# A second edge stage on one Trainium2 core: the order of a group's matrix products on TensorE, and squares in two parts

## The chip, the core and the metric

The kernel runs on one core of one Trainium2 chip. Its time is the device time of one execution in microseconds (us), here the median of three runs. A core has TensorE (PE: matrix products, and PEld: its weight loads), VectorE (DVE), ScalarE (ACT), GpSimd (POOL), SyncE (SP) and DMA engines. Each engine works through its own list of instructions, and the lists meet in semaphores.

## What is computed

The reference is a graph network of two layers over 6250 nodes and 106250 edges. The change lies in the second layer's edge stage alone. Its part of the reference, cut to what matters:

```python
h = silu(edge_scalars @ fc_w1 * (1 / sqrt(8))) * SILU_NORM       # first layer of the edge weights
w = h @ fc_w2 * (1 / sqrt(64))                                   # second layer: 256 weights an edge
w_a, w_b, w_c, w_d = w[:, :64], w[:, 64:128], w[:, 128:192], w[:, 192:]
xg0, xg1 = y0[edge_src], y1[edge_src]                            # gathered rows
mid0 = w_a * xg0 * ea0
mid1 = w_b * einsum('euc,ec->eu', xg1, ea1) * INV_SQRT3
mid2 = (w_c * xg0)[:, :, None] * ea1[:, None, :]
mid3 = (w_d * ea0)[:, :, None] * xg1
agg = segment_sum(concatenate([mid0, mid1, mid2, mid3]), edge_dst)
```

Beside it, in the same stage, run the keys and values of the layer's linear attention: `k, v` of 512 columns each are projected, normalised by their squares' sums, and `dots = k^T v` is summed over all nodes.

## The kernel before

`edges1` runs this stage. 106250 edges are taken in 139 **groups** of 768 edges (six tiles of 128, that is three pairs). The function `turns` writes the first ten groups out, then a loop whose iteration holds ten groups (11 iterations, groups 10 to 119), then the last 19 groups. `q` is a group's place in a turn of five. Groups 0 to 124 also carry a chunk of 250 nodes in five groups: the key and value products (`products`) stand in `q` = 0 to 3, `gram` of the chunk before in `q` = 0 and 2, and none of it in `q` = 4. Groups from 125 on carry no chunk.

In the step of group g each engine does this, in this order:

- **POOL** gathers six tiles of rows three groups ahead, when ACT has copied their indices (`stage`).
- **ACT**: `stage(g+3)`; `attributes(g+1)` (L2084) copies the turned edge scalars out of PSUM; `squares` (L2105, L2109) copies a key or value product out and squares it by head, eight activations each with a read of its accumulator; `copied(g-1)` (L2098) copies the sums of group g-1 to `us`; `silu(g+1)` (L2090); where it is due, `root` (L2114) and `scaled` (L2120). Sqrt and Silu lie in different tables, so that a load of a table stands before the silu that follows a root.
- **DVE**: `eq` (L2192) and `oh` (L2200), the one-hot matrix of the destinations times the attributes; the messages of pair 0, 1 and 2 (L2213 and twice L2215); the three additions of group g-2's step (`add(g-1)`, L2172), after PE's `flip`; the small operations of the normalisation (L2176, L2178, L2183).
- **PE**: `second(g,0)` (L2269, the weight product of pair 0, on 64 rows of the array), `front(g+1)` (L2249, turns the scalars), the first half of `sums(g-1)` (L2283, 24 products of 32 columns), `second(g,1)`, the second half of `sums(g-1)`, `first(g+1)` (L2255), `second(g,2)`, `flip(g-1)` (L2293, which waits for ACT's `us`), then `products` (L2306) and `gram` (L2313).

The weights of pairs 0 and 2 lie in PSUM banks 0 and 1 of `pW`, those of pair 1 in banks 2 and 3, beside `iota` and `eq`. So `second(g,0)` waits until all messages of g-1 are made and until `silu(g)`; `second(g,1)` until `oh(g)` has read `eq`; `second(g,2)` until message 0 of g has read bank 0 and 1. `sums(g-1)` wait for the messages of g-1 and for the additions of g-2.

Of the kernel before, what the change touches and what calls it, by code (L numbers as in the profile page):

```python
# [46 lines left out]
SUB, W1, ST = 3, 32, 2  # L47
# [1913 lines left out]
def edges1(env, z):  # L1961
# [5 lines left out]
    PAIRS = T1 // 2  # L1967
    QW = SUB * W1
    HID = 512
    with ExitStack() as ctx:  # L1970
# [45 lines left out]
        def in_chunks(hi):  # L2016
            return hi < LAST
# [4 lines left out]
        def one_pass():  # L2022
            with nc.Block() as block:
# [49 lines left out]
                @block.scalar  # L2073
                def _(act):
                    def stage(g, s, lo):
                        if lo >= PER:
                            hold(act, s_msg, PAIRS * (g - PER + 1))
                            nc.scalar.copy(ix[:, s, :], srcI[:, bass.ds(g * T1, T1)]).then_inc(s_ix, 1)

                    def attributes(g, s, lo):  # L2080
                        if lo >= 2:
                            hold(act, s_F, g - 1)
                        hold(act, s_T, g + 1)
                        nc.scalar.copy(esT[:, s % 2, :], pT).then_inc(s_esT, 1)  # L2084

                    def silu(g, s, lo):
                        if lo >= 2:
                            hold(act, s_W, PAIRS * (g - 1))
                        hold(act, s_F, g + 1)
                        nc.scalar.activation(hT[:, s % 2, :, :],  # L2090
                                             pH[:, 0:128 * PAIRS].rearrange("p (i e) -> p i e", e=128)[:, :, 0:P],
                                             ACT.Silu, scale=8.0 ** -0.5).then_inc(s_h, 1)

                    def copied(g, lo):
                        if lo >= 1:
                            hold(act, s_flip, g)
                        hold(act, s_acc, g + 1)
                        nc.scalar.copy(us[:, :], pU[0:QW, :]).then_inc(s_us, 1)  # L2098

                    def squares(c, n, lo):  # L2100
                        t, b = n // 2, n % 2
                        if lo >= PER:
                            hold(act, s_gram, 2 * c - 1 + t)
                        hold(act, s_kv, 4 * c + n + 1)
                        nc.scalar.copy((kc, vc)[b][0:R, t, :], pKV[0:R, :]).then_inc(s_cp, 1)  # L2105
                        act.wait_ge(s_cp, 4 * c + n + 1)
                        for h in range(8):
                            head = pKV[0:R, 64 * h:64 * h + 64]
                            last = nc.scalar.activation(head, head, ACT.Square, accum_out=(ssk, ssv)[b][:, t, h:h + 1])  # L2109
                        last.then_inc(s_read, 1)  # L2110

                    def root(c, t):
                        hold(act, s_ab, 2 * c + t + 1)
                        nc.scalar.activation(sd[:, t, :], ab[:, t, :], ACT.Sqrt).then_inc(s_sd, 1)  # L2114

                    def scaled(c, t):
                        hold(act, s_ri, 2 * c + t + 1)
                        hold(act, s_read, 4 * c + 2 * t + 2)
                        for h in range(8):
                            last = nc.scalar.activation(vc[0:R, t, 64 * h:64 * h + 64], vc[0:R, t, 64 * h:64 * h + 64],  # L2120
                                                        ACT.Copy, scale=ri[:, t, h:h + 1])
                        last.then_inc(s_vs, 1)

                    def step(g, r, lo, hi, c):
                        q = r % PER
                        if lo == 0:
                            nc.scalar.activation(ta[0:1, 0:1], env["ones"][0:1, 0:1], ACT.Silu)
                            attributes(0, 0, 0)
                            silu(0, 0, 0)
                        if hi <= GROUPS1 - 4:  # L2130
                            stage(g + 3, (q + 3) % PER, lo + 3)
                        if hi <= GROUPS1 - 2:
                            attributes(g + 1, r + 1, lo + 1)
                        if in_chunks(hi) and q >= 1:
                            squares(c, q - 1, lo)
                        if lo >= 1:
                            copied(g - 1, lo - 1)
                        if hi <= GROUPS1 - 2:
                            silu(g + 1, r + 1, lo + 1)
                        if behind_chunk(lo) and q == 0:  # L2140
                            root(c - 1, 1)
                        if behind_chunk(lo) and q == 1:
                            scaled(c - 1, 1)
                        if in_chunks(hi) and q == 3:
                            root(c, 0)
                        if in_chunks(hi) and q == 4:
                            scaled(c, 0)
                        for n in range(2):
                            if lo == LAST + 7 + 2 * n:
                                act.wait_ge(s_M, n + 1)  # L2150
                                nc.scalar.copy(kc[:, n, :], pKV[:, :]).then_inc(s_m1, 1)
                        if lo == LAST + 11:
                            act.wait_ge(s_G, 1)
                            nc.scalar.copy(env["g0"][:, :, :], pKV[:, :].rearrange("p (k c) -> p k c", k=2))
                        if lo == GROUPS1 - 1:
                            copied(g, lo)
                            act.drain()
                    turns(act, step)

                @block.vector  # L2160
                def _(v):
# [23 lines left out]
                    def step(g, r, lo, hi, c):  # L2185
                        q, s = r % PER, r % 2
# [15 lines left out]
                            in1=ea[:, q, :, :].unsqueeze(3).broadcast_to([P, T1, 4, W1]), op=ALU.mult).then_inc(s_oh, 1)  # L2202
                        bases = []
                        v.wait_ge(s_gat[q], (c + 1) * 16 * T1)
                        for i in range(PAIRS):
                            if lo >= 1:
                                bases.append(base_of(g - 1, i))
                            js = slice(2 * i, 2 * i + 2)
                            v.wait_ge(s_W, g * PAIRS + i + 1)
                            wa = region(i).rearrange("p j (b q c) -> p j b q c", b=2, q=2)  # L2210
                            m = msg[:, s, js, :, :]
                            x0 = rows[:, q, js, 0:64].unsqueeze(2).broadcast_to([P, 2, 2, 64])
                            nc.vector.tensor_tensor(out=m[:, :, 0:8:7, :], in0=wa[:, :, :, 0, :], in1=x0, op=ALU.mult)  # L2213
                            for j in range(2):
                                last = nc.vector.tensor_tensor(  # L2215
                                    out=m[:, j, 1:7, :].rearrange("p (b q) c -> p b q c", b=2), in0=wa[:, j, :, 1:2, :].broadcast_to([P, 2, 3, 64]),
                                    in1=rows[:, q, 2 * i + j, 64:256].rearrange("p (q c) -> p q c", q=3).unsqueeze(1)
                                    .broadcast_to([P, 2, 3, 64]), op=ALU.mult)
                            last.then_inc(s_msg, 1)
# [24 lines left out]
                def _(pe):  # L2244
# [14 lines left out]
                    def second(g, r, lo, i):  # L2259
                        if i == 0:  # L2260
                            pe.wait_ge(s_h, g + 1)
                            if lo >= 1:
                                pe.wait_ge(s_msg, g * PAIRS)
                        elif i == 1:
                            pe.wait_ge(s_oh, g + 1)
                        else:
                            pe.wait_ge(s_msg, g * PAIRS + 1)
                        for n in range(2):
                            last = nc.tensor.matmul(region(i)[:, n, :], hT[64 * n:64 * n + 64, r % 2, i, :],  # L2269
                                                    w2[64 * n:64 * n + 64, :], start=True, stop=True)  # L2270
                        last.then_inc(s_W, 1)
# [67 lines left out]
                    def step(g, r, lo, hi, c):  # L2339
                        q = r % PER  # L2340
                        if lo == 0:
# [2 lines left out]
                                             skip_group_check=True)  # L2344
                            front(0, 0, 0, 0)
                            first(0, 0)
                        second(g, r, lo, 0)
                        if hi <= GROUPS1 - 2:
                            front(g + 1, (q + 1) % PER, lo + 1, c + (1 if q == PER - 1 else 0))
                        if lo >= 1:  # L2350
                            sums(g - 1, r + 1, lo - 1, 0)
                        second(g, r, lo, 1)
                        if lo >= 1:
                            sums(g - 1, r + 1, lo - 1, 1)
                        if hi <= GROUPS1 - 2:
                            first(g + 1, r + 1)
                        second(g, r, lo, 2)
                        if lo >= 1:
                            flip(g - 1)
                        if in_chunks(hi) and q < 4:  # L2360
# [722 lines left out]
```

## Time and profile before

| what | value |
|---|---|
| time, median of 3 runs | 4415.78 us (4412.92 to 4420.58) |
| profiled execution, span from first to last instruction | 3329.5 us |
| median less span | 1086.3 us |
| second edge stage (windows view, from the first `oh` to the last addition) | 1171.54 us |
| busy in the span: PE, PEld, DVE, ACT, POOL | 2844.0, 2195.3, 2255.2, 1469.1, 1823.7 us |
| mean granted clock of PE | 0.935 |

The profile gives no time of its own for the profiled execution besides its span. What lies around the span is taken as 1086.3 us, the median less the span; the change doesn't touch it. In a row of a timeline the first number is the start, the second the duration, both in us, and what stands in brackets is the idle time of the engine before it and what ended it.

### The profile page before, as it was taken

To read this page: it belongs to the slowest core of one execution; us is meant where nothing else is said; L and a number is where in the kernel's file an instruction comes from. 1 tells how busy PE (TensorE), PEld (TensorE's weight loads), DVE (VectorE), ACT (ScalarE), POOL (GpSimd) and SP (SyncE) were. 2 spreads that over 40 slices of the span, in tenths; PEclk is the share of its full clock that TensorE was granted. 3 is DMA by queue.
4 is the path that set the end of the run, shared out by engine and by line. 5 is a ranking of instruction groups with operands and counts; after the bars stand their busy time and mean duration, and the time that the engine had idled before them with its cause. 6 is when DMAs were issued, how large, how long until landed. Compare 5 with 4: busy or idle time off the path is not lost. (4 is left out here: it accounts for less than half of the span.)

```text
span 3329.5 us, 78240 instructions
## 1 busy us (share of the span) xinstructions
PE 2844.0 (85%) x22774; PEld 2195.3 (66%) x22774; DVE 2255.2 (68%) x6176; ACT 1469.1 (44%) x4662; POOL 1823.7 (55%) x1961
## 2 busy tenths in 40 slices
PE   6787878788888788699996999999999999888399
PEld 4576667677777766588884555555555555578387
DVE  5577777777777777576665777777777777768522
ACT  5333333333333157333333665565555556348122
POOL 3577777777777601011115776666666667712254
PEclk9799999999999999899997999999999999999699
DMA  6544444444444557332224444344434444436221
GB/s 183 164 114 112 116 113 113 113 112 117 113 113 118 129 162 198 106 90 83 86 77 113 117 111 104 103 104 103 103 101 103 104 104 110 125 110 200 58 52 47
DMA packets 329958, 375.06 MB, mean 113 GB/s; under 512 B 179225, under 2 KB 236666, under 8 KB 329616
## 3 DMA queue, kind: packets, MB, share of 16 engines
q0 software_dynamic: 89712, 230.26, 25.3%
q1 hardware_dynamic: 238335, 139.99, 16.1%
q10 hardware_dynamic: 1696, 2.62, 0.2%
q14 instruction: 162, 1.32, 0.1%
q8 instruction: 53, 0.87, 0.1%
HBM read 309.90 MB, written 62.84 MB: 112 GB/s over the span
## 5 line engine op out<-in xcount | busy, mean ns | idle before, releaser
L2033 POOL DMA_INDIRECT e_rows<-tab,e_ix x804 | 759.9, 945 | 346.5 <-issue 218.1
L607 POOL DMA_INDIRECT e_rows<-tab,e_ix x805 | 761.3, 946 | 247.5 <-issue 217.2
L1008 PE MATMUL e_pU<-e_ohp,e_rows 128*128 128x128 f32 x3340 | 440.2, 292 | 3.1 <-DVE e_ohp L859 3.1
L1008 PEld LDWEIGHTS e_pU<-e_ohp,e_rows 128*128 128x128 f32 x3340 | 428.5, 209 | 4.8 <-DVE e_ohp L859 3.6
L2215 DVE TENSOR_TENSOR e_msg<-e_pW,e_rows 128x384 f32<-128x384 f32 x834 | 421.5, 547 | 0.0
L2269 PE MATMUL e_pW<-e_w,e_hT 64*128 64x256 f32 x1668 | 324.2, 438 | 76.3 <-DVE e_oh L2200 36.1
L2283 PE MATMUL e_pU<-e_msg,e_oh 128*32 128x128 f32 (+1 forms) x6672 | 374.8, 312 | 8.6 <-DVE sum L2172 7.5
L721 ACT CAST e_ohT<-e_pT 64x640 bf16<-64x640 f32 x167 | 114.4, 685 | 552.1 <-PE e_pT L989 551.8
L2213 DVE TENSOR_TENSOR e_msg<-e_pW,e_rows 128x256 f32<-128x256 f32 x417 | 175.4, 421 | 231.3 <-PE e_pW L2269 222.9
L2283 PEld LDWEIGHTS e_pU<-e_msg,e_oh 128*32 128x32 f32 x6672 | 243.4, 113 | 132.5 <-issue 72.4
L989 PE MATMUL e_pT<-ident,e_oh 128*64 128x128 f32 x835 | 135.5, 299 | 212.0 <-DVE e_oh L514 190.7
L989 PEld LDWEIGHTS e_pT<-ident,e_oh 128*64 128x64 f32 x835 | 89.9, 120 | 252.5 <-issue 248.8
L2269 PEld LDWEIGHTS e_pW<-e_w,e_hT 64*128 64x128 f32 x1668 | 148.3, 193 | 160.4 <-DVE e_msg L2215 64.7
L859 DVE TENSOR_TENSOR e_ohp<-window,e_p 128x1280 f32<-128x1280 f32 x167 | 245.8, 1472 | 0.1
L1699 POOL TENSOR_TENSOR m_rn<-m_ve,m_mhalf 125x2 f32<-125x2 f32 x50 | 45.6, 912 | 336.2 <-DVE m_ve L148 336.2
L2306 PE MATMUL e_pKV<-e_wkv,ffn_norm 128*125 128x512 f32 x400 | 206.2, 641 | 0.0
L1899 PE MATMUL m_pH<-m_xnT,m_w 128*128 128x250 f32 x800 | 175.4, 377 | 6.6 <-DMA m_w<-in_L_ffn_W 6.6
L1912 PE MATMUL m_pO<-m_w,m_hT 128*125 128x256 f32 x800 | 176.7, 379 | 0.0
L828 DVE TENSOR_TENSOR sum<-sum,e_pU 64x128 f32 x334 | 95.6, 286 | 119.4 <-issue 113.5
L2098 ACT COPY e_us<-e_pU 96x512 f32<-96x512 f32 x139 | 80.8, 581 | 213.6 <-PE e_pU L2283 210.3
L1899 PEld LDWEIGHTS m_pH<-m_xnT,m_w 128*128 128x128 f32 x800 | 151.1, 191 | 23.7 <-issue 6.7
L2109 ACT ACTIVATE e_pKV<-e_pKV 125x64 f32<-125x64 f32 x800 | 165.0, 237 | 3.2
(465 smaller groups left out, 5563.9 us busy)
## 6 DMA issues: line engine op xcount, KB each, us to landing
e_rows<-tab,e_ix POOLq DMA_INDIRECT x1609
xnT<-f_xnT SPq DMA_DIRECT2D x25, 250.0 KB, 2.9
e_xk<-xnT SPq DMA_DIRECT2D x25, 250.0 KB
xnT<-b_xT SPq DMA_DIRECT2D x25, 250.0 KB, 2.9
m_xnT<-xnT SPq DMA_DIRECT2D x25, 250.0 KB
xnT<-m_xT SPq DMA_DIRECT2D x25, 250.0 KB, 2.7
ffn_norm<-xnT SPq DMA_DIRECT2D x25, 250.0 KB
tab<-f_hrow SPq DMA_DIRECT2D x25, 227.5 KB
```

The lines of the kernel that those rows point to most:

```text
L607: nc.gpsimd.indirect_dma_start(out=rows[:, s, j, :], out_offset=None, in_=env["tab0"], in_offset=bass.IndirectOffsetOnAxis(ap=at[:, j:j + ...
L859: nc.vector.tensor_tensor(out=ohp[:, s % 3, :, :, :], in0=eq.unsqueeze(2).broadcast_to([P, GT, H0, W]), in1=p[:, s % 3, :, 0:H0].unsqueeze ...
L989: last = nc.tensor.transpose(pT[0:W, P * j:P * (j + 1)], oh[:, s, j, :], ident[:, :])
L1008: nc.tensor.matmul(pU[:, s % 2, 2 * W * k:2 * W * (k + 1)], rows[:, s, j, 128 * k:128 * k + 128], ohp[:, s % 3, j, 2 * k:2 * k + 2, :], st ...
L1899: last = nc.tensor.matmul(pH[:, f // 2, (f % 2) * CH:(f % 2 + 1) * CH], w1[:, j, k, 128 * c:128 * c + 128], xnT[:, s, k, :], start=k == 0, ...
L1912: last = nc.tensor.matmul(pO[:, t * C:(t + 1) * C], hT[:, s % 2, f, t * R:t * R + R], w2[:, f, :], start=f == 0, stop=f == NF - 1)
L2033: nc.gpsimd.indirect_dma_start(out=rows[:, r % PER, j, :], out_offset=None, in_=env["tab1"], in_offset=bass.IndirectOffsetOnAxis(ap=at[:, ...
L2213: nc.vector.tensor_tensor(out=m[:, :, 0:8:7, :], in0=wa[:, :, :, 0, :], in1=x0, op=ALU.mult)
L2215: last = nc.vector.tensor_tensor(out=m[:, j, 1:7, :].rearrange("p (b q) c -> p b q c", b=2), in0=wa[:, j, :, 1:2, :].broadcast_to([P, 2, 3 ...
L2269: last = nc.tensor.matmul(region(i)[:, n, :], hT[64 * n:64 * n + 64, r % 2, i, :], w2[64 * n:64 * n + 64, :], start=True, stop=True)
L2283: last = nc.tensor.matmul(u8[:, 0:8:2, :] if c == 0 else u8[:, 1:2 + 2 * c:2 * c, :], oh[:, r % 2, ST * i + j, c, :], m[:, 0:4, :] if c == ...
L2306: last = nc.tensor.matmul(pKV[0:R, :], xk[:, k, t * R:t * R + R], wkv[:, k, HID * b:HID * b + HID], start=k == 0, stop=k == 1)
```

## The change

On PE the three `second` of a group stand together at its start, in the order of pairs 0, 2, 1, then `front(g+1)`, both halves of `sums(g-1)`, `first(g+1)`, `flip(g-1)`, `products`, `gram`. The waits go with them: pairs 0 and 2 need messages 0 and 2 of g-1, pair 1 needs `oh(g)` and all messages of g-1. DVE makes the messages in the order 0, 2, 1, and waits for the second of PE's signals before the first two. On ACT `squares` is cut into `kept` (the copy) and `squares`; the copy and four heads come before `attributes(g+1)`, the other four after it. No operation is added or removed.

```diff
-                        if hi <= GROUPS1 - 2:
-                            attributes(g + 1, r + 1, lo + 1)
-                        if in_chunks(hi) and q >= 1:
-                            squares(c, q - 1, lo)
+                        chunk = in_chunks(hi) and q >= 1
+                        if chunk:
+                            kept(c, q - 1, lo)
+                            squares(q - 1, range(0, 4))
+                        if hi <= GROUPS1 - 2:
+                            attributes(g + 1, r + 1, lo + 1)
+                        if chunk:
+                            squares(q - 1, range(4, 8)).then_inc(s_read, 1)
...
-                        for i in range(PAIRS):
+                        for done, i in ((2, 0), (2, 2), (3, 1)):
                             if lo >= 1:
-                                bases.append(base_of(g - 1, i))
+                                bases.append(base_of(g - 1, len(bases)))
                             js = slice(2 * i, 2 * i + 2)
-                            v.wait_ge(s_W, g * PAIRS + i + 1)
+                            v.wait_ge(s_W, g * PAIRS + done)
...
                         if i == 0:
                             pe.wait_ge(s_h, g + 1)
                             if lo >= 1:
-                                pe.wait_ge(s_msg, g * PAIRS)
+                                pe.wait_ge(s_msg, g * PAIRS - 1)
                         elif i == 1:
                             pe.wait_ge(s_oh, g + 1)
-                        else:
-                            pe.wait_ge(s_msg, g * PAIRS + 1)
+                            if lo >= 1:
+                                pe.wait_ge(s_msg, g * PAIRS)
...
-                        second(g, r, lo, 0)
+                        for i in (0, 2, 1):
+                            second(g, r, lo, i)
                         if hi <= GROUPS1 - 2:
                             front(g + 1, (q + 1) % PER, lo + 1, c + (1 if q == PER - 1 else 0))
                         if lo >= 1:
-                            sums(g - 1, r + 1, lo - 1, 0)
-                        second(g, r, lo, 1)
-                        if lo >= 1:
-                            sums(g - 1, r + 1, lo - 1, 1)
+                            for j in range(ST):
+                                sums(g - 1, r + 1, lo - 1, j)
                         if hi <= GROUPS1 - 2:
                             first(g + 1, r + 1)
-                        second(g, r, lo, 2)
                         if lo >= 1:
                             flip(g - 1)
```

## Rows read from the trace of the kernel before

**Rows 1.** The page: the span, then two of the costliest groups of instructions.
```profile
span 3329.5 us, 78240 instructions
...
L2269 PE MATMUL e_pW<-e_w,e_hT 64*128 64x256 f32 x1668 | 324.2, 438 | 76.3 <-DVE e_oh L2200 36.1
...
L2109 ACT ACTIVATE e_pKV<-e_pKV 125x64 f32<-125x64 f32 x800 | 165.0, 237 | 3.2
```

**Rows 2.** Windows: stretch, its us, busy time (instructions), PEclk, DMA share, GB/s.
```profile
1779.86:2951.40 1171.54, 1083.55 (x10709) 668.16 (x10709) 853.88 (x2099) 655.64 (x2804) 786.62 (x833) 0.94 0.41 107
2043.53:2118.62 75.09, 70.00 (x730) 43.17 (x728) 55.23 (x138) 48.24 (x215) 51.43 (x55) 1.00 0.42 107
2118.62:2128.86 10.24, 9.44 (x46) 5.60 (x47) 6.57 (x16) 2.65 (x5) 5.37 (x7) 0.50 0.31 79
...
2203.95:2214.19 10.24, 9.44 (x46) 5.59 (x47) 6.57 (x16) 2.65 (x5) 5.56 (x7) 0.50 0.32 81
...
1825.07:1828.48 3.41, 3.29 (x28) 2.02 (x28) 2.66 (x6) 0.90 (x5) 2.50 (x3) 0.50 0.42 103
```

**Rows 3.** Waits of PE in ten iterations (1948 to 2801): in total, times, longest.
```profile
PE e_pW L2269 <- DVE e_oh L2200: 34.8, 20, 3.4
```

**Rows 4.** Timeline of PE: groups 38 and 39, and the start of iteration 40.
```profile
2104.78 0.55 PE L2293 MATMUL e_pU<-ident,e_us 96*128 96x96 f32 x4
2105.16 1.91 PE L2306 MATMUL e_pKV<-e_wkv,ffn_norm 128*125 128x512 f32 x4
...
2107.00 0.70 PE L2269 MATMUL e_pW<-e_w,e_hT 64*128 64x256 f32 x4
...
2107.86 1.29 PE L2283 MATMUL e_pU<-e_msg,e_oh 128*32 128x256 f32 x24
2109.07 0.70 PE L2269 MATMUL e_pW<-e_w,e_hT 64*128 64x256 f32 x4
...
2110.92 0.82 PE L2255 MATMUL e_pH<-e_esT,e_w 48*128 48x128 f32 x5
...
2112.22 0.55 PE L2293 MATMUL e_pU<-ident,e_us 96*128 96x96 f32 x4
2113.85 0.70 PE L2269 MATMUL e_pW<-e_w,e_hT 64*128 64x256 f32 x4 [1.08 <-ACT e_hT L2090]
...
2119.42 1.23 PE L2269 MATMUL e_pW<-e_w,e_hT 64*128 64x256 f32 x4 [3.26 <-DVE e_oh L2200]
```

**Rows 5.** Timeline of ACT and DVE in the same stretch.
```profile
2106.17 1.11 DVE L2172 TENSOR_TENSOR sum<-sum,e_pU 128x128 f32 x3
...
2107.69 0.96 DVE L2200 TENSOR_TENSOR e_oh<-e_pW,e_ea 128x768 f32<-128x768 f32 x1
...
2111.11 0.58 ACT L2098 COPY e_us<-e_pU 96x512 f32<-96x512 f32 x1 [0.53 <-PE e_pU L2283]
2111.94 1.28 ACT L2090 ACT_TABLE_LOAD   x1 [0.25 <-PE e_pH L2255]
...
2113.61 1.11 DVE L2172 TENSOR_TENSOR sum<-sum,e_pU 128x128 f32 x3
...
2118.01 0.36 DVE L2192 TENSOR_TENSOR e_pW<-e_pW,dst_rel 128x192 f32<-128x192 f32 x1 [2.96 <-issue]
2118.41 0.96 DVE L2200 TENSOR_TENSOR e_oh<-e_pW,e_ea 128x768 f32<-128x768 f32 x1
```

**Rows 6.** Timeline of PE and DVE in the middle of an iteration, groups 44 and 45.
```profile
2157.28 0.82 PE L2255 MATMUL e_pH<-e_esT,e_w 48*128 48x128 f32 x5
...
2159.97 1.12 DVE L2172 TENSOR_TENSOR sum<-sum,e_pU 128x128 f32 x3
...
2162.81 0.70 PE L2269 MATMUL e_pW<-e_w,e_hT 64*128 64x256 f32 x4 [0.18 <-DVE e_oh L2200]
```

**Rows 7.** Timeline at the stage's end: both halves of the last sums together, copy, flip.
```profile
2946.11 2.37 PE L2283 MATMUL e_pU<-e_msg,e_oh 128*32 128x256 f32 x48 [2.04 <-DVE sum L2172]
2949.22 0.55 PE L2293 MATMUL e_pU<-ident,e_us 96*128 96x96 f32 x4 [0.74 <-ACT e_us L2098]
...
2948.58 0.58 ACT L2098 COPY e_us<-e_pU 96x512 f32<-96x512 f32 x1 [5.11 <-PE e_pU L2283]
```

More of the change, by code:

```diff
@@ L2098, in copied, with kept @@
                         nc.scalar.copy(us[:, :], pU[0:QW, :]).then_inc(s_us, 1)
-                    def squares(c, n, lo):
+                    def kept(c, n, lo):
                         t, b = n // 2, n % 2
@@ L2106, in squares @@
                         act.wait_ge(s_cp, 4 * c + n + 1)
-                        for h in range(8):
+                    def squares(n, heads):
+                        t, b = n // 2, n % 2
+                        for h in heads:
                             head = pKV[0:R, 64 * h:64 * h + 64]
                             last = nc.scalar.activation(head, head, ACT.Square, accum_out=(ssk, ssv)[b][:, t, h:h + 1])
-                        last.then_inc(s_read, 1)
+                        return last
                     def root(c, t):
```

## The prediction

> **What bounds the kernel now.** I read the page first: the span, and the groups of L2269 and L2109, which the change moves [rows 1]. Then the windows view, to see the stage by itself: 1171.54 us, PE busy in 1083.55 of them, 92%, DVE in 73%; one iteration of the loop is 75.09 us at the full granted clock and 10.24 us at 0.50, 85.33 in all, and the next slow stretch starts 85.33 us after the last (2118.62, 2203.95) [rows 2]. So PE bounds most groups, and what it does not do itself must be sought in its waits. There the longest is for `oh`, 34.8 us in ten iterations [rows 3]. Then the timelines, to see where an iteration loses time.
>
> A group with `products` has no wait on PE. From one start to the next it takes 0.86 (pair 0 and front: 2107.00 to 2107.86), 1.21 (half the sums, to 2109.07), 1.85 (pair 1 and the other half, to 2110.92), 1.30 (first and pair 2, to 2112.22), and, from the group before, 0.38 (flip, 2104.78 to 2105.16) and 1.84 (products, to 2107.00): 7.44 us [rows 4]. A `gram` adds about 0.9 us, which the change leaves alone.
>
> A group with `q` = 4 has no products to cover anything. In group 39, the last of an iteration, PE waits 1.08 us for the silu, which had to load its table (1.28 us), then, past the loop's branch, 3.26 us for the next `oh` [rows 4, 5]. The reason for the second is DVE: it starts its additions at 2113.61, and its list stands still for 2.96 us, waiting for nothing that the profile shows, before 2118.01, the first instruction after the loop's branch [rows 5]. Inside those 3.26 us the granted clock falls to 0.50, for 10.24 us [rows 2].
>
> **The change part by part.** I count from F, the start of `first` in a group, on PE.
>
> Pairs 0, 2, 1 together: a pair takes 0.64, pair 1 and half the sums' 1.85 less the sums' 1.21 [rows 4]. Its own matmuls follow each other as they will in the new order, so three make 1.92, as now. No gain; what a switch between kinds of products could give beyond this is a rival below.
>
> Both halves of the sums together: the last sums of the stage already stand so, 48 products in 2.37 us [rows 7]. Apart a half is 1.21 to the next start and 1.29 to its own end (the row at 2107.86) [rows 4], so both make 2.50. Gain 0.13 a group.
>
> Flip behind first: at present pair 2 stands between them and flip starts at F + 1.30, when ACT's copy of the sums (2111.11 to 2111.69, F + 0.77) has long ended [rows 4, 5]. Now only first, 1.30 - 0.64 = 0.66, stands between. The row at the stage's end gives the wait that is then bare: 0.74 from the sums' end to flip, copy included [rows 7]. The sums end 0.07 after F (1.29 against 1.21), so flip starts at F + 0.81: a new wait of 0.15 on PE, behind which products, gram and the next group are queued. Its bounds are 0 (the switch from first to flip may take that long anyhow) and 0.25.
>
> Sum of a group with products: flip 0.81, products 0.38 + 1.84, pairs 0 and 2 1.28, pair 1 0.64, front 0.22 (0.86 - 0.64), sums 1.21 + 1.21 - 0.13: 7.46 against 7.44, **+0.02 us**. `oh` is not late here: additions to the end of `oh` take 2.48 (2106.17 to 2108.65) [rows 5]. They can start at flip's end plus what lies between in the rows, about 0.14, so at F + 1.50, and end at F + 3.98, while pair 1's turn comes at 0.81 + 0.38 + 1.84 + 1.28 = F + 4.31. The margin is 0.33.
>
> The loop's end: today DVE's additions start at F + 2.69 (2113.61 - 2110.92), because message 2 waits for pair 2. Afterwards they start at F + 1.50, 1.19 earlier, and from them to PE's start behind `oh` it is 5.81 (2113.61 to 2119.42) [rows 4, 5]. So PE resumes at F + 7.31 instead of F + 8.50. But then it has pair 1, front and both halves before the next F, 3.15, where it had 1.85. Together 10.46 against 10.35: **+0.11 us**. What the shorter wait gives, the work no longer done inside it takes back.
>
> The middle of an iteration (`q` = 4 without branch): from the additions to pair 1 it is 2.84 (2159.97 to 2162.81), so pair 1 starts at F + 4.34 and F' = F + 7.49; today it is 5.53 + 1.85 = 7.38 [rows 6]. **+0.11 us**.
>
> ACT: the same operations, four squares ahead of `attributes`. An eight of squares takes under 8 x 0.24 = 1.9 us in a group of 7.4 [rows 1], all of them already stood between front and the copy, and ACT still sat idle 0.53 before the copy [rows 5]. I cost it at 0; if that cover were gone, it is the copy, and with it flip, that would come late by the rest. SP, POOL and the DMAs issue what they issued, at the same places of their lists.
>
> Sum: eight product groups at 0.02 and the two others at 0.11 are 0.38 us an iteration, 4.2 us in 11. The groups before and behind the loop are 29, at 0.02 to 0.11 each, say 1.3. That makes +5.5 us. The profiled span would go from 3329.5 to 3335.0; with the 1086.3 around it, 4421.3. The median was 4415.8.
>
> The clock can change this. PE resumes 0.80 us after the fall begins (2118.62, 2119.42) [rows 2, 4], so 9.44 us of work run at half speed, which costs 4.7. The slow stretches lie exactly 85.33 us apart. If they keep that spacing while an iteration's own work grows a little, the fall begins earlier in PE's pause and covers less work, and the loop gives back some of the 4.2. I take it as the lower half of the forecast's own range, 4414 to 4426.
>
> The Trainium skill ("TensorE: Matmul & The Clock Gate", "Idle/cold" and "Busy/warm" levels) has 1.2 and 2.4 GHz as the two levels. The rows agree, with 0.50 and 1.00.
>
> **The rivals.**
>
> *A second fall of the clock (slower).* Now the pause of a `q` = 4 group is a wait for the silu of 1.08 and then some work on 128 rows before the next wait. Afterwards flip ends at about F + 1.36 and pair 0 starts at F + 2.81 (the silu's 2.93 less 0.12, since first ends earlier with nothing beside it), a wait of 1.45, then only two pairs stand between it and the wait for `oh`. The rows show that one such pause can be enough: at 1825.07 the clock fell for 3.41 us behind group 4 [rows 2], while in the middle of the loop it didn't. It decides as soon as the pause of 1.45 is enough in most iterations where 1.08 was in few. One more fall of 3.41 us an iteration costs 1.7, in 11 iterations 19, together with the 5.5 some 4440. If the fall at the loop's end grew by as much instead, the sum is the same. Against it: the spacing that absorbs small changes. Chance 0.34, with a time of 4426 to 4450.
>
> *Switches cost more than I see (faster).* The order before changes the part of the array in use nine times a group, the new one six. The sums' 0.13 is the one such cost that a row shows. If the two other places from which a pair is taken give 0.13 each, and flip's wait is nothing, a group gains up to 0.39; PE can use it in the 100 groups with products alone, 26 to 39 us, so 4380 to 4395; a half of it gives 4404. In a sentence of its own: the Trainium skill ("TensorEngine Tiling (Array Packing)", "Mode switching requires drain") says that changing the tiling mode drains TensorE, and by it the change gains at each switch that it drops. The trace agrees for the sums, 2.37 against 2.50, and no more than that. Chance 0.16.
>
> *The branch's stop moves (either).* DVE's 2.96 us behind the branch depend on where its list lies. If they vanished, PE would lose neither 3.26 us nor the clock: up to 7.4 us an iteration, 4335. If another engine got one, 4445. The number of instructions in each list hardly changes, so 0.04 for gone, 0.02 for more. The Trainium skill ("Runtime: NRT & Kernel Launch", "Instruction fetch mechanics") says that a taken branch to a page not held forces a fetch; the rows show a stop on DVE's list only.
>
> *It does not do what it says.* If PE's list came out in the old order, 4416. It is a plain reordering; I give it nothing.
>
> **How the numbers follow.** Forecast 0.44, second fall 0.34, switches 0.16, branch 0.06. A measurement of this kernel can tell about 0.2% from no change, 8.8 us, so 4407 to 4424.6. Same: nearly all of the forecast's 0.44, and 0.02 of the switches' case. Slower: 0.34 and 0.02. Faster: 0.14 and 0.04. The time is that of the forecast, 4421. The range is 4396 to 4442: it leaves out the upper end of the second fall (about 0.06), the full switches' case (0.08) and the branch's (0.06).
>
> **What would show it.** Right: in a product group the sums are one block of 2.37 and flip shows a wait of about 0.15 for L2098; PE's wait for `oh` at the loop's end stays near 3.1, with 1.45 for the silu before it; DVE no longer waits for pair 2. The iterations are 85.3 to 85.8 us. Wrong: a slow stretch in the middle of an iteration, a product group under 7.35 or over 7.55, or a wait for `oh` in groups with products.

## The result, and the profile after

The changed kernel took 4446.05 us (4440.81 to 4458.47), the one before 4416.78: ratio 1.0064, 95% interval [1.0046, 1.0082]. It is 29 us slower, where 5.5 were forecast, and lies just above the range of 4396 to 4442.

The page of the changed kernel shows first that the basis of the sum was wrong. Its span is 4438.9 us for a time of 4440.8, so only 2 us lie around a span, not 1086.

```profile
span 4438.9 us, 78158 instructions
...
L2290 PE MATMUL e_pU<-e_msg,e_oh 128*32 128x128 f32 (+1 forms) x6672 | 489.8, 327 | 210.0 <-issue 206.7
...
L2300 PE MATMUL e_pU<-ident,e_us 96*128 96x96 f32 x556 | 105.5, 331 | 140.7 <-ACT e_us L2098 140.0
```

The windows view of three stages (columns as in [rows 2]): first edge stage, FFN, second edge stage; of the changed kernel, then of the trace that stands behind [rows 1] to [rows 7].

```profile
112.00:1605.10 1493.10, 1046.35 (x7398) 884.96 (x7398) 763.05 (x2207) 353.10 (x748) 792.37 (x835) 0.79 0.31 84
1784.50:2197.00 412.50, 384.11 (x1932) 341.07 (x1932) 263.22 (x750) 120.92 (x279) 68.70 (x80) 0.96 0.30 86
2202.00:4057.40 1855.40, 1395.96 (x10711) 859.72 (x10711) 854.76 (x2098) 659.93 (x2806) 790.54 (x834) 0.79 0.26 68
```

```profile
113.50:1181.10 1067.60, 852.25 (x7398) 749.17 (x7398) 768.62 (x2207) 362.64 (x748) 790.37 (x835) 0.94 0.44 117
1360.00:1772.10 412.10, 384.09 (x1932) 340.87 (x1932) 262.95 (x750) 120.68 (x279) 68.65 (x80) 0.96 0.30 86
```

The FFN takes the same time in both. The first edge stage, in which nothing was changed, takes 1493 against 1068 us. So the shown trace of before was most likely taken on another chip than the 4416 us, one where the two edge stages go faster; the experiments bear this out. I name two levels by what the kernel before takes: the **3333 level** (3333 or 3334 us) and the **4416 level** (4416 to 4420 us, on one further chip 4481). Three chips took part in the experiments, and each stayed at one level in all its runs. Why a chip is at one or the other, no run shows. The changed kernel itself never ran at the 3333 level; order_only, which differs from it on ACT alone, stands for it there.

One of the four runs of sums_together_3 below took 6583 us, in a state apart from all others, and is left out.

### The profile page after: what moved, and what is told of

Same layout as the page of the kernel before. It is cut to its first block and busy times, and to the rows that moved or that the text cites. A ratio compares the mean times of both kernels' runs of the same rounds, so it can differ in the third digit from the quotient of the medians.

```text
span 4438.9 us, 78158 instructions
## 1 busy us (share of the span) xinstructions
PE 3347.7 (75%) x22774; PEld 2522.0 (57%) x22774; DVE 2251.3 (51%) x6176; ACT 1463.1 (33%) x4662; POOL 1828.1 (41%) x1961
## 5 line engine op out<-in xcount | busy, mean ns | idle before, releaser
L1008 PE MATMUL e_pU<-e_ohp,e_rows 128*128 128x128 f32 x3340 | 566.8, 328 | 171.2 <-issue 164.4
L2290 PE MATMUL e_pU<-e_msg,e_oh 128*32 128x128 f32 (+1 forms) x6672 | 489.8, 327 | 210.0 <-issue 206.7
L1008 PEld LDWEIGHTS e_pU<-e_ohp,e_rows 128*128 128x128 f32 x3340 | 527.1, 241 | 203.8 <-issue 198.6
L2290 PEld LDWEIGHTS e_pU<-e_msg,e_oh 128*32 128x32 f32 x6672 | 299.3, 118 | 373.7 <-issue 315.8
L2179 DVE TENSOR_TENSOR sum<-sum,e_pU 128x128 f32 x417 | 120.5, 289 | 722.2 <-PE e_pU L2300 681.6
L2276 PE MATMUL e_pW<-e_w,e_hT 64*128 64x256 f32 x1668 | 282.7, 467 | 80.3 <-DVE e_oh L2207 39.1
L2313 PE MATMUL e_pKV<-e_wkv,ffn_norm 128*125 128x512 f32 x400 | 288.0, 860 | 0.0
L837 DVE TENSOR_REDUCE e_lg<-e_pE 128x20 f32<-128x60 f32 x167 | 35.5, 213 | 429.8 <-remote 409.3
L2300 PE MATMUL e_pU<-ident,e_us 96*128 96x96 f32 x556 | 105.5, 331 | 140.7 <-ACT e_us L2098 140.0
L2262 PE MATMUL e_pH<-e_esT,e_w 48*128 48x128 f32 x834 | 174.7, 341 | 27.7 <-issue 25.5
```

What stands on the lines that cost most here:

```text
L1008: nc.tensor.matmul(pU[:, s % 2, 2 * W * k:2 * W * (k + 1)], rows[:, s, j, 128 * k:128 * k + 128], ohp[:, s % 3, j, 2 * k:2 * k + 2, :], st ...
L2262: last = nc.tensor.matmul(pH[:, P * i:P * (i + 1)], w1[:, i, :], esT[:, r % 2, :], start=True, stop=True)
L2290: last = nc.tensor.matmul(u8[:, 0:8:2, :] if c == 0 else u8[:, 1:2 + 2 * c:2 * c, :], oh[:, r % 2, ST * i + j, c, :], m[:, 0:4, :] if c == ...
L2313: last = nc.tensor.matmul(pKV[0:R, :], xk[:, k, t * R:t * R + R], wkv[:, k, HID * b:HID * b + HID], start=k == 0, stop=k == 1)
```

## The experiments

The ratio is to the kernel before on the same chip. It is estimated over all runs (2 to 10 of each kernel), so it can differ by 0.001 from the quotient of the medians.

| kernel | level (us of before) | median us | ratio, 95% interval |
|---|---|---|---|
| order_only | 3332.8 | 3339.0 | 1.0019 [1.0007, 1.0030] |
| squares_only | 3332.8 | 3332.5 | 1.0002 [0.9991, 1.0013] |
| after_again | 4416.8 | 4445.3 | 1.0077 [1.0057, 1.0098] |
| sums_together | 4416.8 | 4449.5 | 1.0082 [1.0066, 1.0099] |
| sums_parted | 4416.8 | 4461.7 | 1.0105 [1.0088, 1.0122] |
| third_halved | 4481.1 | 4406.5 | 0.9835 [0.9815, 0.9854] |
| half_products | 4481.1 | 4466.7 | 0.9966 [0.9951, 0.9981] |
| sums_together_2 | 4481.1 | 4514.9 | 1.0071 [1.0055, 1.0088] |
| after_third | 4481.1 | 4511.8 | 1.0064 [1.0047, 1.0081] |
| pair2_up | 4420.4 | 4407.9 | 0.9972 [0.9959, 0.9985] |
| sums_in_three | 4420.4 | 4448.4 | 1.0055 [1.0035, 1.0076] |
| sums_together_3 | 4420.4 | 4444.7 | 1.0064 [1.0040, 1.0088] |
| after_fourth | 4420.4 | 4454.0 | 1.0084 [1.0061, 1.0107] |
| sums_then_pair1 | 3334.3 | 3237.9 | 0.9710 [0.9694, 0.9726] |
| pair2_up_squares | 3334.3 | 3291.2 | 0.9877 [0.9849, 0.9906] |
| pair2_up_again | 3334.3 | 3295.2 | 0.9892 [0.9869, 0.9915] |

**Two levels: before_again and before_third** are the kernel before, unchanged.

> The kernel before, unchanged, profiled once more. Its shown profile has a span of 3329.5 us and a time of 4415.8; the changed kernel's profile has 4438.9 with a time of 4440.8, so its span holds nearly all of the time. Theory A (the shown profile of before is of an execution that ran without stops that the timed ones have): the span comes out near 4414, the second edge stage near 1830 us instead of 1172, and the first edge stage, which nothing changes, near 1490 instead of 1068. Theory B (some 1086 us lie outside the span): the span comes out near 3330 again.

It took 3333.73 us with a span of 3331.9, which neither theory had put so: the span does hold nearly all of the time, so no 1086 us lie outside it and B falls, but this chip is at the other level. Then, on a chip at the 4416 level:

> The kernel before, unchanged, for a profile on the chip that the other three of this call run on. Two levels of this kernel have been seen: 4416 us and 3333 us, each steady on its chip. Theory A (on some chips PE's instructions come with stops): if the time is near 4416, the rows of both halves of sums show idle time put down to issue, which they don't show at 3333, and the loads of instructions in the loop are as few as in the first profile (53) or a whole loop of them. Theory B (the changed kernel alone has such stops, because its loop's code no longer stays loaded): at 4416 too the sums of this kernel would run unbroken.

It took 4417.51 with a span of 4415.6 and 53 loads on the instruction queue. Theory A holds, B falls: the unchanged kernel has the long edge stages and the stops too. Its first and second edge stage in the windows view:

```profile
112.20:1604.70 1492.50, 1057.79 (x7398) 896.87 (x7398) 762.42 (x2207) 352.29 (x748) 791.74 (x835) 0.78 0.31 84
2201.90:4033.10 1831.20, 1394.76 (x10711) 805.45 (x10711) 861.47 (x2098) 655.54 (x2806) 790.04 (x834) 0.80 0.26 69
```

Timeline of PE, ACT and DVE in group 39:

```profile
2739.60 0.70 PE L2269 MATMUL e_pW<-e_w,e_hT 64*128 64x256 f32 x4
2740.23 1.05 PE L2283 MATMUL e_pU<-e_msg,e_oh 128*32 128x256 f32 x15
2742.24 0.27 PE L2283 MATMUL e_pU<-e_msg,e_oh 128*32 128x128 f32 x1 [0.95 <-issue]
2742.96 0.27 PE L2283 MATMUL e_pU<-e_msg,e_oh 128*32 128x128 f32 x1 [0.46 <-issue]
...
2747.23 0.58 ACT L2098 COPY e_us<-e_pU 96x512 f32<-96x512 f32 x1 [6.12 <-PE e_pU L2283]
...
2746.59 0.42 DVE L2213 TENSOR_TENSOR e_msg<-e_pW,e_rows 128x256 f32<-128x256 f32 x1 [6.16 <-remote]
```

In the second half of the sums PE stops, then runs one product every 0.7 us. Pair 1, started at 2739.60, is over by 2740.30 in this view, yet DVE, which waits for nothing but its signal, starts only at 2746.59, as PE's stop ends. So at this level not only do PE's instructions come late, what waits for them is released late too. Ends of products are modelled in this view, so it doesn't tell a late signal from a product that ended late. Neither the stops nor the late releases are in the trace that I argued from, and what causes them was not tested.

**The two parts of the change: order_only and squares_only.**

Edits, shortened; a line with `#` says what the kernel starts from.

```diff
+# order_only: the changed kernel, but on ACT
+                        if hi <= GROUPS1 - 2:
+                            attributes(g + 1, r + 1, lo + 1)
+                        if in_chunks(hi) and q >= 1:
+                            squares(c, q - 1, lo)
+# squares_only: the kernel before, with the changed kernel's kept, squares and their places
```

> PE's and DVE's new order, with squares undivided and behind attributes, as before. If the order is the cause of the slowdown: within 0.2% of the changed kernel, 4440 to 4455 us. If the early squares are the cause (attributes and with it first come later): near 4416 us. With the squares undivided the copy of the sums may come late: its row would then show a later start after the sums, and the time would lie above 4450.

> The old order of PE and DVE, squares in two parts with four heads ahead of attributes. If the order is the cause: 4412 to 4422 us. If the squares are: 4435 to 4450 us.

Both ran at the 3333 level, so of what was expected only the ratios can be held against them. The order costs 6.2 us (1.0007 to 1.0030) and for the squares no difference shows. That is close to the forecast's 5.5, but by luck: the terms are others. Timeline of PE in order_only, a product group without wait and the middle of an iteration:

```profile
2238.17 0.70 PE L2269 MATMUL e_pW<-e_w,e_hT 64*128 64x256 f32 x4 [0.33 <-DVE e_oh L2200]
...
2241.33 0.93 PE L2255 MATMUL e_pH<-e_esT,e_w 48*128 48x128 f32 x6
...
2244.26 1.13 PE L2269 MATMUL e_pW<-e_w,e_hT 64*128 64x256 f32 x8 [1.46 <-ACT e_hT L2090]
2246.36 0.79 PE L2269 MATMUL e_pW<-e_w,e_hT 64*128 64x256 f32 x4 [0.96 <-DVE e_oh L2200]
...
2255.07 1.57 PE L2269 MATMUL e_pW<-e_w,e_hT 64*128 64x256 f32 x12
2256.57 0.29 PE L2249 MATMUL e_pH<-ident,e_es 128*48 128x128 f32 x1
2256.79 2.38 PE L2283 MATMUL e_pU<-e_msg,e_oh 128*32 128x256 f32 x48
2259.09 0.93 PE L2255 MATMUL e_pH<-e_esT,e_w 48*128 48x128 f32 x6
2260.10 0.55 PE L2293 MATMUL e_pU<-ident,e_us 96*128 96x96 f32 x4
...
2262.32 1.61 PE L2269 MATMUL e_pW<-e_w,e_hT 64*128 64x256 f32 x12
```

Three pairs together take 1.50 us (2255.07 to 2256.57), not 1.92. The two halves take 2.30, not 2.29. Flip stands at F + 1.01, not 0.81. The group is 7.25, not 7.46 us. The wait for the silu is 1.46, as forecast. In the middle PE waits 0.96 for `oh`, where the kernel before had 0.18 [rows 6]; it also waits 0.33 us for `oh` behind the products of `q` = 3, twice an iteration, where it had no wait. And the clock falls a second time: the windows of order_only, two falls at the loop's end and two in the middle of an iteration.

```profile
2202.47:2209.30 6.83, 6.07 (x46) 3.33 (x45) 5.17 (x11) 0.45 (x2) 4.48 (x5) 0.50 0.39 98
2246.85:2250.26 3.41, 3.41 (x33) 2.03 (x34) 3.27 (x8) 0.26 (x1) 2.77 (x3) 0.50 0.48 113
2287.81:2294.64 6.83, 5.81 (x44) 3.09 (x45) 5.17 (x11) 0.28 (x2) 4.72 (x5) 0.50 0.40 101
2332.18:2335.59 3.41, 3.41 (x33) 1.99 (x34) 3.26 (x8) 0.26 (x1) 2.75 (x3) 0.50 0.46 108
```

6.83 and 3.41 are the 10.24 of before [rows 2], cut in two, and these two iterations still lie 85.34 us apart (falls at 2202.47 and 2287.81).

Where do the 6.2 us lie, then? The windows view split at the `oh` of group 120, the first behind the loop: before_again, loop and the 19 groups behind it, then order_only.

```profile
1868.15:2794.40 926.25, 864.15 (x8505) 530.57 (x8502) 678.48 (x1673) 560.06 (x2420) 632.17 (x669) 0.95 0.42 106
2794.40:2947.27 152.87, 134.42 (x1474) 86.91 (x1468) 114.86 (x279) 50.55 (x177) 90.78 (x96) 0.96 0.39 103
```

```profile
1866.21:2795.01 928.80, 844.11 (x8518) 555.75 (x8516) 682.10 (x1672) 551.69 (x2421) 631.39 (x668) 0.94 0.42 107
2795.01:2953.43 158.42, 134.13 (x1478) 91.33 (x1475) 114.41 (x279) 51.41 (x181) 91.71 (x97) 0.94 0.38 100
```

The loop, where I had put 4.2 of my 5.5 us, shows no loss: 928.80 us against 926.25 here, 932.14 in the first trace and 933.07 in squares_only. Behind the loop it is 158.42 against 152.87, and the old order has 152.86 to 152.88 in all three traces. PE's wait for `oh` in that stretch, before_again, then order_only:

```profile
PE e_pW L2269 <- DVE e_oh L2200: 0.9, 2, 0.7
```

```profile
PE e_pW L2269 <- DVE e_oh L2200: 15.8, 15, 2.2
```

Most of these groups carry no products, so nothing covers the way from flip over the additions to `oh` when pair 1 stands ahead of both halves. The 15 us more for `oh` are set off in part by shorter waits for messages and additions (8.2 and 5.0 us before, none and 1.5 after).

**The halves together, alone: sums_together; and parted by front: sums_parted.** All of these ran at the 4416 level.

```diff
+# sums_together: the kernel before, with
                         second(g, r, lo, 1)
                         if lo >= 1:
+                            for j in range(ST):
+                                sums(g - 1, r + 1, lo - 1, j)
+# sums_parted: the changed kernel, with sums(.., 0), front(g + 1), sums(.., 1)
```

> The changed kernel once more. On a chip at the 3333 level: my own sum of +5.5 us holds, a ratio of 1.001 to 1.003, as order_only gave (1.0019). On a chip at the 4416 level: 1.0064 again, 1.005 to 1.008.

> The kernel before with both halves of the sums together behind pair 1, and pair 2 left between first and flip; nothing else is moved. My terms: 0.13 us a group gained, no bare wait before flip, so 10 to 15 us faster at the 3333 level (ratio 0.995 to 0.998). If long unbroken runs of short products are what costs at the 4416 level, it is as slow there as the changed kernel, 1.004 to 1.008; if the bare wait before flip and the pairs are, it is 1.000 or below there too.

> The changed kernel with front moved between the halves of the sums. My terms: the 0.13 us a group is lost again, all else stays, so 10 to 15 us slower than the changed kernel at the 3333 level (ratio to before 1.005 to 1.008). If long unbroken runs are the cost at the 4416 level, part of the 1.0064 is given back there, 1.002 to 1.005.

After_again repeats the loss, as expected. Sums_together has all of it (repeated twice: 1.0071, 1.0064), without the moved pair 2 and without the bare wait before flip, so these are not needed for the loss. Sums_parted was expected at 1.002 to 1.005 and is worse than the changed kernel, for a reason of its own: front comes later, and PE waits 120.6 us for the copied scalars before first. It decides nothing on the length of the sums. Waits of PE in the second edge stage: before_third, then sums_together_3.

```profile
PE e_pU L2283 <- issue: 186.9, 274, 2.4
PE e_pU L2293 <- ACT e_us L2098: 171.6, 47, 6.0
...
PE e_pW L2269 <- DVE e_oh L2200: 14.0, 7, 2.2
```

```profile
PE e_pU L2283 <- issue: 249.3, 370, 3.1
PE e_pW L2269 <- DVE e_oh L2200: 92.3, 64, 4.3
PE e_pU L2293 <- ACT e_us L2098: 39.7, 23, 4.4
```

Two idle times grow, the stops inside the sums by 62 us and the wait for `oh`, now ahead of both halves, by 78; the wait before flip shrinks by 132.

Split as above, the windows of before_third (loop, then the 19 groups behind it), and of the changed kernel in after:

```profile
2352.81:3813.62 1460.81, 1127.10 (x8517) 648.23 (x8514) 684.69 (x1672) 558.74 (x2421) 625.11 (x660) 0.80 0.26 67
3813.62:4034.37 220.75, 164.96 (x1477) 100.72 (x1471) 116.32 (x279) 49.53 (x175) 90.92 (x96) 0.83 0.27 71
```

```profile
2352.90:3832.50 1479.60, 1120.62 (x8518) 687.99 (x8516) 680.01 (x1673) 561.43 (x2421) 625.46 (x660) 0.80 0.26 66
3832.50:4058.70 226.20, 169.39 (x1480) 109.17 (x1476) 114.83 (x279) 51.22 (x180) 90.98 (x96) 0.81 0.26 69
```

Behind the loop the loss is 5.4 us, the same as at the 3333 level. The rest of what these two traces differ by lies in the loop, 18.8 us here, and 12 and 22 in after_again and after_fourth.

**Work or instructions: third_halved and half_products.** Each leaves a part of the sums or products out. Both ran on the chip where the kernel before takes 4481 us; no trace of the kernel before was taken there.

```diff
-                            for i in range(SUB):
+                            for i in range(SUB - j):
...
-                        for k in range(2):
+                        for k in range(1):
```

> The kernel before with the third of three sub-blocks left out of the second half of the sums, so its sums lack that part. This takes 16 of some 160 instructions a group off PE's list (2224 of 22575 in the stage, 9.9%) and next to no time off its array, since three sub-blocks run beside each other. Theory A (at the 4416 level PE's instructions come at a limited rate, 22575 in 1831 us, 12.3 a us): the stage shrinks by a tenth there, some 180 us, to a time near 4235. Theory B (the stops are of fixed number and length): the stage stays near 1831. At the 3333 level both say: 0 to 8 us faster.

> The kernel before with the second of two contractions left out of every key and value product, so keys and values lack half their sum. This takes about 0.92 us of work off PE in each of 100 groups, but only 400 of its 22575 instructions. Theory A: at the 4416 level the instructions set the pace, so it gives 400/12.3 = 33 us, 4385; theory B: the 92 us of work and more at the lower clock, 4325 or less. At the 3333 level DVE's chain takes over, 35 to 80 us faster.

2224 instructions less gave 74.5 us, 34 ns each; 400 less, with 92 us of PE's work, gave 14.4. Neither theory gave the size: for the first, the steady rate would give 180 and the fixed stops 8. The second can't be read as a price of work: it ran at a mean granted clock of 0.75 in the stage, against 0.80 in before_third. Added up from the clock records of the traces, that is 904 us at half speed against 713. The 191 us more can cost up to 95, as much as the work that was left out. So less work on PE was largely paid back by its clock, as far as two chips can be compared.

**Which half of the move: pair2_up and sums_in_three, then sums_then_pair1.** Shortened to the order of PE's list in a step:

```diff
+# pair2_up: order_only, with
+                        second(g, r, lo, 0)
+                        second(g, r, lo, 2)
                         front, sums(g - 1, .., 0)
+                        second(g, r, lo, 1)
                         sums(g - 1, .., 1), first, flip
+# sums_then_pair1: second 0, 2, front, both sums, second 1, first, flip
+# sums_in_three: the kernel before, second 0, front, 3 parts, second 1, 3 parts, second 2, 2 parts, first, flip
```

> Pairs 0 and 2 together at the start, then front, first half of the sums, pair 1, second half, first, flip; DVE's order 0, 2, 1; squares undivided. The halves stay parted by pair 1, as before. If unbroken sums are the cause at the 4416 level: 0.999 to 1.003 there. If moving pair 2 and the bare wait before flip are: 1.005 to 1.008. At the 3333 level: my terms give a bare wait of 0.15 us a product group and no 0.13 gained, less 1.2 us of DVE's wait at the loop's end, 1.000 to 1.005.

> The kernel before with the eight parts of the sums cut 3, 3, 2, parted by pair 1 and pair 2, and first behind the last part. If runs of short products drain PE's instructions at the 4416 level, shorter runs drain them less: 0.992 to 0.999 there. If not: 1.000 to 1.006 from the wait before flip, now 1.30 us less covered. At the 3333 level 1.001 to 1.006: one switch more and the wait before flip bare.

Pair2_up keeps the moved pair 2 and the bare wait before flip and is 12.5 us faster than before at the 4416 level. From it to the changed kernel, 0.9972 to 1.0084 on one chip, two things change: pair 1 stands ahead of the first half, and the squares are in two parts. That the first one costs, sums_together shows in the old order; what the squares do at this level was not measured. At the 3333 level pair2_up was expected at 1.000 to 1.005 and came to 0.9892: there too my terms missed a gain, of 39 us.

Sums_in_three has shorter runs and less idle time put down to issue in the sums (135.7 against 186.9 us) and is 28 us slower all the same. But the idle time put down to issue at all lines of PE is the same, about 219 against 217 us: it moved to the products behind the sums (first 46.2, pairs 37.3). So shorter runs did not take the stops away.

The next two were meant for the 4416 level:

> As pair2_up, with pair 1 moved behind both halves: the 48 products of the sums unbroken, but no longer behind the wait for the one-hots. If the unbroken run is the cause at the 4416 level: 1.005 or more, with the idle time put down to issue in the sums above 200 us. If the wait ahead of both halves is: below 1.001. At the 3333 level: 0.13 us a group gained against pair2_up.

> pair2_up with the changed kernel's squares in two parts, so the changed kernel with pair 1 put back between the halves. The squares did nothing at the 3333 level (1.0002). At the 4416 level: within 0.003 of pair2_up's 0.9972; if it is at 1.005, the squares carry part of the loss.

Both ran on a chip at the 3333 level, so their questions for the 4416 level stay open. What sums_then_pair1 shows instead is large: 0.9710, 57 us less than pair2_up_again, where 0.13 us a group, 18 in all, was expected. Timeline of PE in sums_then_pair1, a product group and group 40, behind the loop's branch:

```profile
2075.62 1.14 PE L2269 MATMUL e_pW<-e_w,e_hT 64*128 64x256 f32 x8
2076.69 0.29 PE L2249 MATMUL e_pH<-ident,e_es 128*48 128x128 f32 x1
2076.91 2.38 PE L2283 MATMUL e_pU<-e_msg,e_oh 128*32 128x256 f32 x48
2079.21 0.70 PE L2269 MATMUL e_pW<-e_w,e_hT 64*128 64x256 f32 x4
2079.75 0.83 PE L2255 MATMUL e_pH<-e_esT,e_w 48*128 48x128 f32 x6
...
2082.73 1.14 PE L2269 MATMUL e_pW<-e_w,e_hT 64*128 64x256 f32 x8
...
2094.15 0.70 PE L2269 MATMUL e_pW<-e_w,e_hT 64*128 64x256 f32 x4 [0.80 <-DVE e_oh L2200]
```

The group takes 7.11 us against 7.44: pairs 0 and 2 in 1.07, pair 1 in 0.54. Both halves now lie between flip and the need for `oh`, so that its wait in this iteration is 0.80 where it was 3.26 [rows 4]. In the whole stage it is

```profile
PE e_pW L2269 <- DVE e_oh L2200: 4.4, 4, 1.6
```

against 36.1 us in the kernel before and 50.2 in order_only. The stage in order_only, then in sums_then_pair1:

```profile
1779.20:2952.20 1173.00, 1057.92 (x10711) 697.41 (x10711) 856.60 (x2098) 648.23 (x2806) 788.48 (x834) 0.94 0.42 108
1777.00:2854.00 1077.00, 1007.21 (x10711) 694.26 (x10711) 847.75 (x2098) 645.32 (x2806) 789.06 (x834) 0.97 0.46 117
```

Of the 96 us, 45 are idle time of PE, about what the wait for `oh` lost. The other 51 are busy time with the same products. By an estimate 14 of them come from 100 groups of 7.11 instead of 7.25, and the rest goes with the higher clock, 0.97 instead of 0.94. This version beats the kernel before and order_only at the 3333 level; at the other it wasn't run. Pair2_up beats the kernel before at both levels, and the changed kernel or order_only with it. With the squares in two parts it is at 0.9877 instead of 0.9892, and the intervals overlap: no difference shown.

## Why the prediction was wrong

1. *The basis.* I set "with the 1086.3 around it" beside a span of 3329.5 and went on. That was the step that failed most. There is no such time around the span: 2 us lie there in every run whose span is on record. The time and the trace were of different levels, and the 1086 us lie inside the stages, 660 of them in the second edge stage (1831 against 1171). Every term of the sum was read from a trace without the stops and late releases of the 4416 level. There the change costs 29 us, not 5.5.
2. *"The groups before and behind the loop are 29, at 0.02 to 0.11 each, say 1.3".* The 19 behind it cost 5.5 us at both levels (152.87 to 158.42, 220.75 to 226.20). Fourteen of them have no products, and the margin for `oh` that I had worked out for a product group isn't there. The loop, put at 4.2, shows nothing at the 3333 level. So the agreement of +6.2 with +5.5 is luck.
3. *Pairs together, "No gain".* Mis-sized: 1.50 against 1.92, a gain of 0.42 us a group. A pair's 0.64 holds a part that a block of pairs pays once: four products take 0.64 us, eight 1.07, twelve 1.50, so some 0.21 for each block that is dropped. The rival on switches had this right; that its gain doesn't show is the next point.
4. *"The margin is 0.33".* It was smaller than what PE had gained. Waits for `oh` come to 50.2 us in 63 places in order_only, against 36.1 in 23 before. Much of the gain on PE became a wait for DVE's chain from flip to `oh`. In the middle of an iteration pair 1 starts at F + 5.03 (2241.33 to 2246.36), where I had F + 4.34.
5. *Flip's bare wait* was sized too small: F + 1.01 in the group shown and F + 0.92 in the next, against F + 0.81.
6. *The loop's end*, "the work no longer done inside it takes back": the mechanism is right, and sums_then_pair1 shows it from the other side. With the same products and the wait for `oh` behind both halves the kernel is 3.1% faster than order_only (0.9710 against 1.0019 of before), about half of it idle time of PE.
7. *The second fall* happened in order_only, at 2246.85 and 2332.18, which I had named as a sign of being wrong, as I had a product group under 7.35 and a wait for `oh` with products ahead of it. But it didn't add the 19 us: the fall at the loop's end shrank from 10.24 to 6.83 by as much. I had given it the price without the other's change. That the measured 4446 lies in this rival's 4426 to 4450 is luck.
8. *The branch's stop* stayed: 11 stops of some 3 us on DVE's list in order_only (32.4 us). But PE got one too, to which I had given 0.02 ("if another engine got one"): in order_only 125 loads stand on the instruction queue against 53 to 62 before, and in 8 of the 11 iterations PE waits 3.3 to 3.7 us, put down to issue, at the loop's start. At 2287.32 this lay in a pause that was there anyway: pair 1 resumed at F + 7.76, where it was F + 8.50 before. At the 4416 level it isn't the cause: sums_together loses as much with 62 to 71 loads, and pair2_up gains with 98.
9. *The 4416 level*: shown is that joining the two halves behind pair 1 and its wait is enough for the loss, and that 5.4 us of it lie behind the loop as at the other level. For the 12 to 22 us in the loop the cause is open. In the stage the changed kernel has 25 us more of wait for `oh` than before_third (39 to 40 against 14.0), 11 to 28 more of stops in the sums (198 to 215 against 187), and 22 to 45 less of the wait before flip. The clock is a third candidate: added up from the clock records, its low stretches are 744 to 754 us against 713, and 676 in pair2_up. None of the three was changed alone at this level.

## What to carry to other kernels

Hold the profile's span against the timed median before anything else. Here they differed by 2 us when trace and times were of one level and by 1086 when they weren't, and then the trace's gaps were not those of the timed runs. A wait for a slow chain should stand behind the independent work of its engine: the same products in another order gave 1.0019 and 0.9710. A gain on one engine counts only as far as the margin of the chain that meets it there. And cost the groups outside the loop by themselves when they lack work that covers a wait inside it.

## What was not expected of the hardware

- The same kernel takes 3333 or 4416 us by the chip, with the FFN stage at 412 us on both and the edge stages 1068 and 1172 against 1492 and 1831. Why is open.
- At the slower level PE stops within runs of short products, going on at one product in 0.7 us, and DVE was released 6 us after the product that it waited for had ended in the view.
- There 2224 instructions less on PE were worth 34 ns each, and 92 us of products less gave 14.4 us, while the mean granted clock went to 0.75.
- Products of 64 rows take 0.125 us each when twelve follow each other, 0.134 when eight do, and 0.16 in a block of four between sums.
- The falls of the clock go from one of 10.24 us an iteration to 6.83 and 3.41 with the same sum. Most iterations of the kernel before and the later ones of order_only take 85.0 to 85.5 us although their groups differ (7.44 and 7.25 us). The period isn't fixed, though: in pair2_up_again iterations take 81 to 84 us and in sums_then_pair1 75 to 83.
